# Attention block on one core: V made one step behind the scores, eight steps to a turn, both residuals added first

## What is computed

```python
q = _heads(x @ Wq + bq); k = _heads(x @ Wk + bk); v = _heads(x @ Wv + bv)
scores = jnp.einsum('bhqd,bhkd->bhqk', q, k) / np.sqrt(64)
bias = jnp.where(adj, 0.0, NEG)[:, None]
probs = jax.nn.softmax(scores + bias, axis=-1)
ctx = jnp.einsum('bhqk,bhkd->bhqd', probs, v)
y = x + ctx.reshape(128, 128, 384) @ Wf + bf
out = (y - mean(y)) / sqrt(var(y) + 1e-5)
```

## Time and profile before

| | us |
|---|---|
| median of 3 runs | 1088.62 (1088.13 to 1091.04) |
| the profiled execution | 1088.34 |
| its span in the profile | 1086.6 |
| granted clock of TensorE, mean share of full speed | 0.996 |

### The profile page before, as it was taken

How to read it: one execution, slowest core, us unless ns; L and a number is a source line. 1 busy time by engine, 2 the same in 40 slices (tenths; PEclk the granted TensorE clock), 3 DMA queues, 4 the chain that set the end, 5 groups by cost and what they waited for, 6 DMA issues and landing times.

```text
span 1086.6 us, 26751 instructions
## 1 busy us (share of the span) xinstructions
PE 1031.7 (95%) x7161; PEld 903.0 (83%) x7161; DVE 741.7 (68%) x2823; ACT 593.1 (55%) x2119; POOL 635.0 (58%) x652
## 2 busy tenths in 40 slices
PE   8999999999999999999999999999999999999985
PEld 7888888888888888888888888888888888888874
DVE  3677767766776777677677677767766776776665
ACT  4664654654655655645546546556556456465452
POOL 1355565565566656656655655655566566556566
PEclk9999999999999999999999999999999999999998
DMA  7256656666665656656656656656566666564444
GB/s 196 69 159 177 173 165 183 183 178 175 176 168 167 176 167 171 163 172 162 176 164 170 164 169 171 170 166 175 166 170 172 169 166 167 173 165 148 140 138 133
DMA packets 338970, 179.63 MB, mean 165 GB/s; under 512 B 222592, under 2 KB 322560, under 8 KB 338944
## 3 DMA queue, kind: packets, MB, share of 16 engines
q1 hardware_dynamic: 338544, 178.74, 59.5%
q10 hardware_dynamic: 400, 0.59, 0.1%
HBM read 103.75 MB, written 75.50 MB: 165 GB/s over the span
## 4 chain that ended last, share of the span: by engine, by line
PE 33%; ACT 31%; issue 18%; DVE 15%; DMA 1%; POOL 1%; ACTq 1%; DVEq 1%; SPq 0%; POOLq 0%
ACT probs L623 22%; PE scores_ps L354 9%; PE cov_ps L368 8%; DVE y_sb L532 5%; PE cov_ps L338 5%; ACT kT L641 5%; PE cov_ps L340 4%; PE cov_ps L339 4%; DVE xT_lo L489 4%; DVE stats L535 3%; ACT xT_hi L610 2%; ACT qT L641 2%; PE qk_ps L338 1%; PE qk_ps L339 1%; PE qk_ps L340 1%
## 5 line engine op out<-in xcount | busy, mean ns | idle before, releaser
L623 ACT ACTIVATE probs<-s_mask,neg_max 128x128 f32<-128x128 f32 x768 | 297.4, 390 | 5.5 <-DVE neg_max L506 5.5
L500 DVE CUSTOM_DVE_ANT_0 s_mask<-scores_ps,mask_bias 128x128 f32<-128x128 f32 x768 | 172.5, 287 | 134.4 <-PE scores_ps L354 126.2
L714 POOL TENSOR_TENSOR probs<-probs,inv_sum 128x768 f32<-128x768 f32 x128 | 188.9, 1476 | 80.0 <-DVE inv_sum L519 80.0
L709 POOL TENSOR_SCALAR y_sb<-y_sb,mean_var,rstd 128x384 f32<-128x384 f32 x127 | 209.8, 1652 | 23.4 <-POOL rstd L703 23.4
L512 DVE STREAM_TRANSPOSE p_turned<-probs 128x768 f32<-128x768 f32 x128 | 125.2, 978 | 116.2 <-POOL probs L714 116.1
L338 PE MATMUL cov_ps<-wv_hi,xT_hi 128*128 128x384 f32 x384 | 133.5, 348 | 35.1 <-DVE y_sb L532 33.5
L703 POOL TENSOR_TENSOR rstd<-var_eps,minus_half 128x1 f32<-128x1 f32 x128 | 71.9, 562 | 157.1 <-DVE var_eps L541 153.7
L632 ACT COPY v_sb<-cov_ps 128x384 f32<-128x384 f32 x128 | 61.3, 479 | 176.2 <-PE cov_ps L340 176.2
L641 ACT ACTIVATE qT<-qk_ps,bq_col 128x512 f32<-128x512 f32 x96 | 65.5, 682 | 154.4 <-PE qk_ps L340 154.4
L623 ACT ACTIVATION_READ_ACCUMULATOR probs<-s_mask,neg_max 128x1 f32 x768 | 144.8, 189 | 0.0
L690 POOL TENSOR_SCALAR mask_bias<-adj_u 128x128 f32<-128x128 uint8 x128 | 38.1, 298 | 172.2 <-issue 86.8
(11 more groups left out here) (57 smaller groups left out, 2090.8 us busy)
## 6 DMA issues: line engine op xcount, KB each, us to landing
p_out<-p_turned SPq DMA_DIRECT2D x128, 384.0 KB, 2.3
pT<-p_out SPq DMA_DIRECT2D x512, 96.0 KB, 2.2
x_in<-in_x SPq DMA_DIRECT2D x128, 192.0 KB, 2.6
out<-y_sb SPq DMA_DIRECT2D x128, 192.0 KB, 2.2
x_blocks<-in_x SPq DMA_DIRECT2D x360, 64.0 KB, 2.3
adj_u<-in_adj SPq DMA_DIRECT2D x32, 64.0 KB, 2.2
y_sb<-in_L_gnn_Wq ACTq DMA_DIRECT2D x1, 576.0 KB, 4.7
s_mask<-in_L_gnn_Wk SPq DMA_DIRECT2D x1, 576.0 KB, 6.1
```

Source lines behind the costliest of these rows:

```text
L500: last = nc.vector.tensor_tensor_reduce(out=s_mask[:, e, h, :], in0=scores_ps[:, score_cols(e, h)], in1=mask_bias[:, e, :], scale=SCALE, s ...
L623: last = nc.scalar.activation(probs[:, e, h, :], s_mask[:, e, h, :], ACT.Exp, bias=neg_max[:, e, h:h + 1], scale=1.0, accum_out=row_sum[:, ...
L709: nc.gpsimd.tensor_scalar(y_sb[:, y, :], y_sb[:, y, :], mean_var[:, e, 0:1], rstd[:, e, 0:1], ALU.subtract, ALU.mult).then_inc(y_ready, 1)
L714: nc.gpsimd.tensor_tensor(probs[:, e, :, :], probs[:, e, :, :], inv_sum[:, e, :].unsqueeze(2).broadcast_to([P, HEADS, SEQ]), ALU.mult).the ...
```

## The change

- `v_product` in step p makes V of pair p-1 (`V_LAG` = 1) and not of pair p+2. V of a pair is then made in the step after its scores and used in the step after that, as before in the step after it was made. So no V is made before step 1, and V of pairs 61, 62 and 63 is made in steps 62, 63 and 64. `xT_hi` and `xT_lo` hold four groups (`XT_RING` = 4), since a sequence's x is now kept until its V is made.
- A ring of four groups takes eight steps to come round, so a turn of the hardware loop has eight steps (`TURN` = 8): 12 steps written out, 6 turns, and the rest written out (for SP 5 turns).
- DVE adds the residual of both sequences (`add_residual`) before the statistics of either (`find_stats`).
- The bias row is made in bank `cov_ps[0]`. The first V product waits for it, no longer the first scores. The rest of Wv is computed after the rest of Wf.
- SP issues the load of `adj` ahead of the stores of y, without a wait of its own.

```diff
-TURN = 4
+TURN = 8
+V_LAG = 1
+XT_RING = 4
+TURN_GROUPS = TURN * 2 // GROUP
...
-        xT_hi = sb("xT_hi", [P, 2, KC, GTOK], F32R)
-        xT_lo = sb("xT_lo", [P, 2, KC, GTOK], F32R)
+        xT_hi = sb("xT_hi", [P, XT_RING, KC, GTOK], F32R)
+        xT_lo = sb("xT_lo", [P, XT_RING, KC, GTOK], F32R)
...
+                if c % 2 == 0 and real(p + 2, PAIRS):
+                    g, slot = TURN_GROUPS * i + c // 2 + 1, (c // 2 + 1) % 2
+
+                    sp.dma_start(adj_u8[:, slot, :, :],
+                                 adj[bass.ds(g * GROUP, GROUP), :, :].rearrange("b q k -> q b k")
+                                 ).then_inc(adj_loaded[slot], DMA)
                 if real(p - STORE_LAG, PAIRS):
...
-                if c % 2 == 0 and real(p + 2, PAIRS):
-                    g, slot = 2 * i + c // 2 + 1, (c // 2 + 1) % 2
-                    past(sp, masked_ready, 2 * (p - 1) + 1)
...
                     if isinstance(n, int) and n == 0:
                         past(pe, xT_split, BY_MATMUL - 1)
-                        pe.wait_ge(bias_row_ready, 1)
...
-                if isinstance(p, int) and p - 1 + AHEAD >= PAIRS:
-                    past(pe, y_added, n - 2)
-                else:
-                    past(pe, v_copied, 2 * (p - 1 + AHEAD) + e)
+                past(pe, v_copied, n)
...
             def v_product(c, p, e):
-                n, at = 2 * (p + AHEAD) + e, 2 * (c + AHEAD) + e
-                par, tok = at // GROUP % 2, tokens(at)
+                n, at = 2 * (p - V_LAG) + e, 2 * (c - V_LAG) + e
+                par, tok = at // GROUP % XT_RING, tokens(at)
...
                 if real(p - LAG, PAIRS):
                     past(pe, y_added, 2 * (p - LAG) + e)
-                else:
-                    past(pe, v_copied, n - 2)
+                elif e == 0:
+                    pe.wait_ge(bias_row_ready, 1)
...
-                past(pe, xT_split, GROUP)
                 for k in range(KC):
-                    last = nc.tensor.matmul(xT_bank(0)[:, 0:HID], bv_wide[:, k, :], w_raw["f"][:, k, :],
+                    last = nc.tensor.matmul(cov_ps[0][:, 0:HID], bv_wide[:, k, :], w_raw["f"][:, k, :],
                                             start=k == 0, stop=k == KC - 1)
...
-                if early and p == -2:
-                    split_weight("v")
                 if early and p == -1:
                     dve.wait_ge(bias_mm, 1)
-                    nc.vector.tensor_tensor(bias_row[:, :], xT_bank(0)[:, 0:HID], bf_row[:, :], ALU.add
+                    nc.vector.tensor_tensor(bias_row[:, :], cov_ps[0][:, 0:HID], bf_row[:, :], ALU.add
                                             ).then_inc(bias_row_ready, 1)
                     split_weight("f")
+                    split_weight("v")
                 if real(p - LAG, PAIRS):
-                    residual_and_stats(i, c, 0, 2 * (p - LAG))
+                    for e in range(2):
+                        add_residual(i, c, e, 2 * (p - LAG) + e)
+                    find_stats(c, 0, 2 * (p - LAG))
                 if real(p, PAIRS):
                     turn_blocks(i, c, 1, 2 * p + 1)
                 if real(p - LAG, PAIRS):
-                    residual_and_stats(i, c, 1, 2 * (p - LAG) + 1)
+                    find_stats(c, 1, 2 * (p - LAG) + 1)
...
-                past(act, qk_done, 2 * i + at // GROUP - 2, per=NJ)
-                past(act, v_done, n - 2 * GROUP)
+                past(act, qk_done, TURN_GROUPS * i + at // GROUP - XT_RING, per=NJ)
+                past(act, v_done, n - XT_RING * GROUP)
...
-                if real(p + AHEAD, PAIRS):
-                    for e in range(2):
-                        copy_v(c, e, 2 * (p + AHEAD) + e)
+                if real(p - V_LAG, PAIRS):
+                    for e in range(2):
+                        copy_v(c, e, 2 * (p - V_LAG) + e)
```

More of the change, by code:

```diff
@@ L254, in load_x_blocks @@
             def load_x_blocks(i, c, half):
-                g = 2 * i + (c + BLOCKS_AHEAD) // 2
+                g = TURN_GROUPS * i + (c + BLOCKS_AHEAD) // 2
                 slot = (c + BLOCKS_AHEAD) // 2 % 2
@@ L374, in qk_product @@
                 mat, m = QK_JOBS[j]
-                g, par = 2 * i + (c + AHEAD) // 2, (c + AHEAD) // 2 % 2
+                g, par = TURN_GROUPS * i + (c + AHEAD) // 2, (c + AHEAD) // 2 % XT_RING
                 if isinstance(g, int) and g == 0:
@@ L519, in invert_sums, with add_residual @@
                 nc.vector.reciprocal(inv_sum[:, e, :], row_sum[:, e, :]).then_inc(sum_inverted, 1)
-            def residual_and_stats(i, c, e, n):
+            def add_residual(i, c, e, n):
                 at = 2 * (c - LAG) + e
@@ L530, in residual_and_stats, with find_stats @@
                 else:
-                    dve.wait_ge(y_stored[y], (2 * i + at // Y_RING) * DMA)
+                    dve.wait_ge(y_stored[y], (2 * TURN // Y_RING * i + at // Y_RING) * DMA)
                 nc.vector.tensor_tensor(y_sb[:, y, :], cov_ps[e][:, 0:HID], x_bias[:, at % X_RING, :], ALU.add
                                         ).then_inc(y_added, 1)
+            def find_stats(c, e, n):
+                y = (2 * (c - LAG) + e) % Y_RING
                 past(dve, y_added, n)
@@ L628, in copy_v @@
             def copy_v(c, e, n):
-                slot = (2 * (c + AHEAD) + e) % V_RING
+                slot = (2 * (c - V_LAG) + e) % V_RING
                 past(act, v_done, n)
@@ L636, in copy_qk @@
                 mat, m = QK_JOBS[j]
-                g, par = 2 * i + (c + AHEAD) // 2, (c + AHEAD) // 2 % 2
+                g, par = TURN_GROUPS * i + (c + AHEAD) // 2, (c + AHEAD) // 2 % 2
                 past(act, qk_done, g * NJ + j)
@@ L686, in make_mask_bias @@
                 par = at // GROUP % 2
-                past(pool, adj_loaded[par], i + at // (2 * GROUP), per=DMA)
+                past(pool, adj_loaded[par], TURN_GROUPS // 2 * i + at // (2 * GROUP), per=DMA)
                 past(pool, max_found, n - 2)
@@ L694, in add_bias @@
                 slot = (2 * c + e) % X_RING
-                past(pool, x_loaded[slot], i, per=DMA)
+                past(pool, x_loaded[slot], 2 * TURN // X_RING * i + (2 * c + e) // X_RING, per=DMA)
                 past(pool, y_added, n - X_RING)
```

9 lines of the change are left out of this document (3 added, 6 removed).

## The result

The changed kernel took 1099.2 us (median of 4 runs, 1097.56 to 1100.87), the one before 1089.66 beside it (median of 4, 1088.13 to 1091.04): a ratio of 1.0088, 95% interval 1.0065 to 1.0111. The forecast of 1051.9 was 47.3 us too low, and the sign was wrong. (0.9% is little, but the two sets of runs don't overlap.)

A forecast was written before the change was run, and what follows sets the result against it. PE was taken to bound the steps, with one hole in each from DVE's order. Against 1088.34 us: -44.9 - 7.3 - 0.2 + 4.7 + 11.0 = -36.7, so 1051.6, as a median 1051.9 us; range 1037 to 1062.

The forecast's parts named there:

- PE bounds the steps and DVE's order puts a hole in each: Inner steps: PE sets the pace, and waiting for the residual sum of e=1 leaves it a 0.78 us hole each step.
- The term of 44.9 us: Steps 2 to 59: both sums first gives 15.73 us a step, 912.3 against 957.26 us, so -44.9 us.
- The rival that it would, 0.2 us a step: Inner steps: the sum of e=0 comes 0.2 us later each step, V waits 11.6 us more, 1063.5 us; chance 0.12.
- The start, -7.3: Up to the first scores: waiting for Wv and two V products leave PE's path, -7.3 us (bounds -8.2 and -5).
- the end, +4.7: From step 62 on: V of pairs 61 to 63 now lies there, +4.7 us (bounds +2 and +8).
- Steps 0 and 1: First two steps: they lose V on PE, but DVE's list of 11.1 us takes over: -0.1 each, -0.2 us.
- The sum without fetches: Whole kernel: the eight-step text stays on the core, so the 11 us drop out, 1040.9 us; chance 0.23.
- The text of eight steps doesn't stay, and each jump waits for a fetch: Loop jumps: doubled text is likelier not to stay; 2.2 us for each of PE's 5 jumps, +11.0 us.
- What it loads is used a step or more later: nothing: SP's queue in inner steps: it waits 1.4 us for DVE's turning, so reordered stores and loads cost nothing.
- between 200 and 900 us: Sign: instruction packets in this time, with a 2 to 3 us hole one step in eight, if the text doesn't stay.
- The slower rival: Whole loop: text streams and PE waits for every 16 KB block, 92 us on 1040.9, so 1133 us; chance 0.03.
- Only a smaller memory than PE's is outgrown: Loop jumps: only a memory like DVE's overflows, its fetches cost 5 us in all, 1045.9 us; chance 0.12.

## Why the prediction was wrong, and where it was right

*PE bounds the steps and DVE's order puts a hole in each.* Right. The term of 44.9 us for 58 steps is 957.26 - 58 x 15.68 = 47.8 where SP keeps up (the bound of 47.6 in the prediction is 0.2 short), since the sum of e=0 did not come late. The rival that it would, 0.2 us a step, is out.

*The start, -7.3, and the end, +4.7.* Right: first scores at 26.29 (forecast "near 26"), last stretch 47.64 (forecast 47.0). Steps 0 and 1 took 1.5 more than forecast; with no loop and SP relieved they took 22.26 (26.45 to 48.71), as forecast. The sum without fetches was 1040.9, and the kernel without jumps and with SP relieved took 1039.0. That these are so near is in part luck: the steps were 0.05 us shorter than forecast, 3 us in all, and the end 0.6 longer.

*The text of eight steps doesn't stay, and each jump waits for a fetch.* Right in kind and nearly in size: +11.0 forecast, 14 measured. But it was built of a wrong piece. I took one wait of 2.2 us on PE. The traces show a branch of 3.6 to 4.4 us on PE, which shows as 1.0 in PE's matmuls, and 4.59 us of nothing on DVE, which costs a second time. With the loop begun at an unlucky place it was 7.2 a jump (turns of 8 alone). That the total came near is thus partly luck. The Trainium skill, "Runtime: NRT & Kernel Launch", section "Instruction fetch mechanics", has a taken branch to a block outside a window of two force a fetch before execution goes on. The runs agree that such a jump waits, 3.6 to 4.4 us on PE's branch; they don't agree with the window, as the 4-step turn is longer than that and its branch took 0.21 us.

*"What it loads is used a step or more later: nothing."* This is the step that failed: the term for SP was put at nothing. I read SP's slack from its wait for DVE, 131.7 / 95 = 1.4 us, and called the queue free. That is the mean of one wait over the whole span, start and end included; in the inner steps it was 1.0 a wait and 1.80 a round. I never added up a round of SP in a step of 15.7. It measured 15.55 us with the sums first, 0.12 below the step. The hole in PE's step had been SP's room as well: removing it took about 0.8, and the waits for landings grew by 0.87, which no sum over the rows of before would have shown. Then I priced the streaming at the jump alone. The forecast itself had fetches "between 200 and 900 us" as a sign, but nothing asked who shares the way with them. 67 packets of 16 KB stretch SP's issues, 43.5 us in 700 by count, and that was more than the room. This way went 45.9 us, as the run with ACT's loads shows. Beside it the jumps were 3 more than forecast and the steps, at 15.68, 3 less, so that nearly all of the 46.6 us too much in steps 2 to 61 is SP's.

*The slower rival* (chance 0.03) had the right cause, text that streams, but the wrong victim. It let PE wait for each block, and on that ground I ruled it out, because step 60 has a packet and is packed. PE indeed never waited for a block of straight text: the kernel with no loop and SP relieved has 58 packets and steps of 15.68. Its rule, 3.7 blocks a turn waited for, decides nothing here. What decides is SP's 0.12 us of free time a step.

*Only a smaller memory than PE's is outgrown.* Both PE's and the others' were: q14 went from 15 packets to 105.

What stays open: why a packet stretches an issue. That they fall together, and cost together, is shown by counts and by the run that adds PE's packets alone; whether they share a ring, an engine or a port wasn't tried. Why fewer issues are stretched once ACT has the loads is open as well. The median landing of the stores of `p_out` also varies: 2.3 us in the three kernels in which SP waits for DVE in nearly every step (before, the change with ACT's loads, and V one ahead with ACT's loads), and 2.6 to 3.2 in all others. So the landing goes with whether SP pauses ahead of its stores; the cause was not tried.

## What to carry to other kernels

When an engine's hole is closed, add up the full round of every queue that serves it, issues and landing waits together, against the new step: a wait that is seen there is no slack for a step that shrinks. Leave a margin beyond the sum, since the landings can grow too: here 1.80 us of waiting shrank to 0.12 for a step only 0.8 us shorter. A loop's length is a resource of its own. While its text stays on the core, a turn costs nothing seen; once it doesn't, as with turns of 8 here, the whole text is fetched on every turn, and the price is paid at the jumps of several engines and by whatever issues transfers. Take a change with several parts apart: here the part that gains (49 us) needed none of the part that lost it.

## What the runs showed of the hardware that I had not expected

- A jump to text that is not on the core takes 3.6 to 4.4 us on PE (median branch; 0.21 us when it is there), and a second wait of 3.16 us followed in one layout of the program; four more instructions ahead of the loop took it away. Granted clock of 0.50 for 3.4 to 10.2 us came behind these waits.
- A packet of 16 KB of PE's instructions went with an issue of SP that took about 1 to 1.4 us longer (34.4 us over 36 issues; 1.36 and 1.43 in the two shown).
- A queue's waits for landings are not fixed: for the same stores SP waited 3.97, 4.84 and 4.26 us a round in three kernels (before, with the sums first, and with the loads in halves).
- Text written out in full, 58 packets for 7161 matmuls, made PE wait nowhere from step 2 to step 61 (busy 940.82 of 940.82 us): streaming straight ahead was free for the engine that ran it, and not for the queue beside it.
